# Sparse layer of a fused two-block network: inner rows and second weights as scaled 2-byte pairs, rows turned by DMA, tiles in two halves

## The reference

```
x = x + L0_xattn(layernorm(x), ctx)
xf = layernorm(x)                                   # 2048 x 512
inter = xf @ c1_w.T @ c2_w.T                        # 512 -> 16 -> 1792
idx = argmax of each block of 32 columns of inter   # 56 blocks a row
h = relu(xf . w1[idx])                              # one kept number per block
x = x + sum over the blocks of h * w2t[idx]
x = x + L1_xattn(layernorm(x), ctx)
x = x + L1_gated_ffn(layernorm(x))
```

## Time and profile before

| | |
|---|---|
| median of three runs | 1622.94 us |
| the profiled execution | 1623.3 us, of which the span from first to last instruction is 1621.5 us |
| granted TensorE clock, mean | 0.987 of full speed |
| TensorE matmul busy | 1553.2 us (96%) |
| VectorE busy | 1175.9 us (73%) |
| ScalarE busy | 812.9 us (50%) |
| GpSimd busy | 597.4 us (37%) |
| first attention (with the layer's first matmuls) | 0 to about 183 us |
| sparse layer, TensorE | about 183 to 553 us |
| second attention and gated layer | 554 to 1621.5 us |

### The profile page before, as it was taken

How to read it: one execution, slowest core, us unless ns; L and a number is a source line. 1 busy time by engine, 2 the same in 40 slices (tenths; PEclk the granted TensorE clock), 3 DMA queues, 4 the chain that set the end, 5 groups by cost and what they waited for, 6 DMA issues and landing times.

```text
span 1621.5 us, 28847 instructions
## 1 busy us (share of the span) xinstructions
PE 1553.2 (96%) x11178; PEld 970.2 (60%) x11178; DVE 1175.9 (73%) x2200; ACT 812.9 (50%) x2496; POOL 597.4 (37%) x570
## 2 busy tenths in 40 slices
PE   5999799999999878999999999999999999999998
PEld 4878566767666644555555655655555555555554
DVE  4886787878877768767667667667667667667777
ACT  5678411010011465656646656656656656656753
POOL 5668641212212133333324334334333333334343
PEclk9999899999999989999999999999999999999999
DMA  7432130000000121122121121121122122111102
GB/s 232 155 112 92 65 143 1 1 1 0 1 1 1 54 59 46 34 85 57 29 61 50 31 66 51 29 66 53 29 64 57 29 61 56 30 27 31 24 21 105
DMA packets 124073, 85.45 MB, mean 53 GB/s; under 512 B 108592, under 2 KB 108720, under 8 KB 121248
## 3 DMA queue, kind: packets, MB, share of 16 engines
q1 hardware_dynamic: 122640, 76.27, 17.4%
q10 hardware_dynamic: 1296, 7.34, 1.3%
HBM read 54.22 MB, written 4.19 MB: 36 GB/s over the span
## 4 chain that ended last, share of the span: by engine, by line
PE 44%; DVE 8%; ACT 8%; DMA 3%; POOL 2%; issue 1%; DVEq 0%
PE bank L73 13%; PE bank L75 13%; PE bank L74 13%; ACT a_prob L1632 5%; DMA a_pT_lo<-a_p_lo 3%; PE bank L2239 2%; ACT bank L1603 1%; POOL a_prob L1509 1%; DVE a_qT_lo L1836 1%; DVE a_p_lo L1889 1%; PE bank L2213 1%; DVE x_res L1832 1%; DVE a_nmx L1877 1%; DVE a_q_lo L1841 1%; PE bank L2214 1%
## 5 line engine op out<-in xcount | busy, mean ns | idle before, releaser
L1632 ACT ACTIVATE a_prob<-a_prob,a_nmx 128x64 f32<-128x64 f32 x512 | 170.2, 333 | 232.9 <-DVE a_nmx L1877 232.9
L73 PE MATMUL bank<-w,a_oT_hi 128*128 128x512 f16 x512 | 196.7, 384 | 7.0 <-DVE a_oT_lo L1895 6.9
L74 PE MATMUL bank<-w,a_oT_lo 128*128 128x512 f16 x512 | 196.5, 384 | 0.0
L75 PE MATMUL bank<-w,a_oT_hi 128*128 128x512 f16 x512 | 196.3, 383 | 0.0
L1832 DVE SCALAR_TENSOR_TENSOR x_res<-bank,a_oinv,x_res 128x512 f32<-128x512 f32 x128 | 95.7, 748 | 132.6 <-PE bank L75 132.4
L73 PE MATMUL bank<-a_big 128*128 128x512 f32 (+1 forms) x416 | 166.5, 400 | 13.2 <-DVE a_big L729 8.5
L1017 ACT CAST a_big<-bank 128x512 fp32r<-128x512 f32 x64 | 34.0, 532 | 270.3 <-PE bank L1194 270.2
L1509 POOL TENSOR_TENSOR a_prob<-a_prob,a_mask 128x512 f32<-128x512 f32 x64 | 79.9, 1271 | 240.6 <-DVE a_prob L1871 240.6
L75 PE MATMUL bank<-a_big 128*128 128x512 f32 (+1 forms) x416 | 157.3, 378 | 0.0
L975 POOL TENSOR_TENSOR a_wide<-a_wide 128x448 bf16<-128x448 bf16 x64 | 66.4, 1037 | 246.4 <-DVE a_wide L1064 246.4
L74 PE MATMUL bank<-a_big 128*128 128x512 f32 (+1 forms) x416 | 156.7, 377 | 0.0
(11 more groups left out here) (342 smaller groups left out, 4261.2 us busy)
## 6 DMA issues: line engine op xcount, KB each, us to landing
shared<-in_l_wq SPq DMA_DIRECT2D x8, 1024.0 KB, 4.9
shared<-in_l_wo SPq DMA_DIRECT2D x8, 1024.0 KB, 5.2
shared<-in_w ACTq DMA_DIRECT2D x8, 896.0 KB, 4.5
a_wide<-in_l_ctxT SPq DMA_DIRECT2D x16, 256.0 KB, 2.8
x_res<-in_x SPq DMA_DIRECT2D x16, 256.0 KB, 4.0
shared<-in_ctx SPq DMA_DIRECT2D x16, 256.0 KB, 3.7
shared<-in_l_wkv SPq DMA_DIRECT2D x8, 512.0 KB, 3.9
out_x<-x_res SPq DMA_DIRECT2D x16, 256.0 KB, 2.1
```

The costliest lines, as they stand in the source:

```text
L73: pe.matmul(out, a_hi, b_hi, start=first, stop=False)
L74: pe.matmul(out, a_lo, b_hi, start=False, stop=False)
L75: return pe.matmul(out, a_hi, b_lo, start=False, stop=last)
L1632: ins = act.activation(pt, pt, ACT.Exp, bias=nmx[:, col:col + 1], accum_out=den[:, col:col + 1])
```

## The change

1. h is no longer split after the turning but before it: ScalarE makes a 2-byte high part from h in SBUF (`hidden_hi`), GpSimd the low part (`hidden_lo`), and SP turns both with DMA transposes of 128 x 896 (`hidden_T`), two halves of a tile, so four a tile. The 14 TensorE transposes, the copy out of PSUM and VectorE's low part go.
2. w2 becomes a scaled 2-byte pair. Its largest magnitude is found during the first attention: w2 is loaded once more in 7 pieces (SP), VectorE reduces one piece in each of bodies 6 to 12, spreads and turns the maximum in bodies 12 and 13 (one TensorE transpose) and makes the scale. Each piece then gets a scaling pass on ScalarE before its split; pieces 0 and 1 are scaled and split in front of the last exponential of the first attention.
3. The next chunk's rows are normalised and cut into 2-byte pairs in SBUF (ScalarE, GpSimd) and turned by SP's DMA transposes, one tile at a time (`rows_T`, `rows_hi`, `rows_lo`). The 16 TensorE transposes a chunk and VectorE's `dve_norm` and `dve_lo` for them go. `low_rank` runs per tile of 128 columns instead of per chunk.
4. TensorE's order: a tile has two halves, two quarters of hidden, then a half of the previous product with w2, then two score matmuls (loop below). The four banks freed give hidden three banks instead of two.
5. Scales: xf in this layer is scaled by 4 and w1 to 8 instead of 1024 and 16384, so that h fits 2 bytes; the second attention keeps its own.
6. The loads of the next layer's weights are issued after tile 1's transposes, in the same SP queue.

```diff
-        w2_hi, w2_lo = l0.big[:, 0:NI * D], l0.big[:, NI * D:2 * NI * D]
+        w2_hi, w2_lo = sb("w2_hi", [P, NI * D], F16), sb("w2_lo", [P, NI * D], F16)
+        hT_hi, hT_lo = sb("hT_hi", [P, NI, P], F16), sb("hT_lo", [P, NI, P], F16)
+        h_hi, h_lo = sb("h_hi", [P, INTER], F16), sb("h_lo", [P, INTER], F16)
+        xr_hi, xr_lo = sb("xr_hi", [P, TPC, D], F16), sb("xr_lo", [P, TPC, D], F16)
-        i_banks, h_banks, hT_banks, o_banks = bank[0:2], bank[2:4], bank[4:6], bank[6:8]
+        i_banks, h_banks, o_banks = bank[0:2], bank[2:5], bank[6:8]
 # SP
+            def hidden_T(n, e):
+                if n:
+                    sp.wait_ge(s_og, 2 * (n - 1) + e + 1)
+                sp.wait_ge(s_hh, n * NQ + 2 * e + 2)
+                sp.dma_start_transpose(hT_hi[:, e * NH:(e + 1) * NH, :], h_hi[:, half_cols(e)]).then_inc(s_hT[e], 16)
+                sp.wait_ge(s_hl, n * NQ + 2 * e + 2)
+                sp.dma_start_transpose(hT_lo[:, e * NH:(e + 1) * NH, :], h_lo[:, half_cols(e)]).then_inc(s_hT[e], 16)
+            def rows_T(c, t):
+                k, rows = c * TPC + t, slice(t * P, (t + 1) * P)
+                if k:
+                    sp.wait_ge(s_xT, 32 * k)
+                sp.wait_ge(s_h, (k + 1) * NQ)
+                sp.wait_ge(s_xrh, k + 1)
+                sp.dma_start_transpose(m.xT_hi[:, :, rows], xr_hi[:, t, :]).then_inc(s_xT, 16)
+                sp.wait_ge(s_xrl, k + 1)
+                sp.dma_start_transpose(m.xT_lo[:, :, rows], xr_lo[:, t, :]).then_inc(s_xT, 16)
+            for n in range(NT):
+                c, t = n // TPC, n % TPC
+                hidden_T(n, 0)
+                if t == TPC - 2:
+                    rows_T(c, 0)
+                    rows_T(c, 1)
+                if t == TPC - 1:
+                    rows_T(c, 2)
+                hidden_T(n, 1)
+                if t == TPC - 1:
+                    rows_T(c, 3)
+                if n == 1:
...
 # GpSimd
+            def hidden_lo(n, q):
+                if n:
+                    pool.wait_ge(s_hT[q // 2], 32 * n)
+                pool.wait_ge(s_hh, n * NQ + q + 1)
+                pool.tensor_tensor(h_lo[:, quarter(q)], h[:, quarter(q)], h_hi[:, quarter(q)], ALU.subtract).then_inc(s_hl, 1)
...
 # ScalarE
+            def hidden_hi(n, q):
+                if n:
+                    act.wait_ge(s_hT[q // 2], 32 * n)
+                act.wait_ge(s_hm, n * NQ + q + 1)
+                act.copy(h_hi[:, quarter(q)], h[:, quarter(q)]).then_inc(s_hh, 1)
...
 # VectorE
+            for n in range(NT):
+                c, t = n // TPC, n % TPC
+                select(n, 0)
+                select(n, 1)
+                if TPC <= n + 1 < NT:
+                    low_lo(n + 1, bass.ts((n + 1) % TPC, P), low_bank[32:64, 0:P])
...
+                if 2 <= n < NT - 1:
+                    add_out(n - 1)
+                find_max(n, 2)
+                find_max(n, 3)
...
+                select(n, 2)
+                select(n, 3)
+                if n + 1 < NT:
+                    find_max(n + 1, 0)
+                    find_max(n + 1, 1)
 # TensorE
+            for n in range(2, NT - 1):
+                hidden(n, 0)
+                hidden(n, 1)
...
+                if n + 1 >= TPC:
+                    low_rank(n + 1)
+                out_half(n - 1, 1)
+                block_scores(n, 2)
+                block_scores(n, 3)
...
+                hidden(n, 2)
+                hidden(n, 3)
+                block_scores(n + 1, 0)
+                block_scores(n + 1, 1)
...
+                out_half(n, 0)
 # the first attention
+            if n in MAX2_AT:
+                w2_largest(MAX2_AT[n])
+            if n == 12:
+                w2_spread()
+            if n == 13:
+                w2_scales()
+            if n == NT - 1:
+                before_exps()
```

More of the change, by code:

```diff
@@ L266, in l0_attention @@
     MAX_AT = {n: n - 1 for n in range(1, 5)}
+    MAX2_AT = {n: n - 6 for n in range(6, 13)}
     SPLIT_AT = {n: n - 7 for n in range(7, 15)}
@@ L1186, in _ @@
+            ins.then_inc(m.wql_ok, 1)
+            add_out(NT - 1)
         @block.tensor
         def _(pe):
[L1188 to L1195 removed]
@@ L1197, in out_rows, with block_scores @@
-            def out_rows(n, g, odd, free=True, split=False):
-                pe.wait_ge(s_hTl, n * NQ + g + 1)
-                if split:
-                    pe.wait_ge(wl_ok, -(-TG[g].stop * D // PW))
-                if free and g == 0:
+            def block_scores(n, q):
+                if q == 0:
+                    pe.wait_ge(s_lowl, low_turn(n))
+                if n or q >= 2:
+                    pe.wait_ge(s_eq, n * NQ + q - 1)
+                pe.matmul(i_banks[q % 2][:, 0:QC], low[:, bass.ts(n % TPC, P)], c2st[:, quarter(q)], start=True,
+                          stop=True).then_inc(s_i, 1)
@@ new lines, in hidden @@
+            def hidden(n, q):
+                e, rows = n * NQ + q, bass.ts(n % TPC, P)
+                if n >= TPC and q == 0:
+                    pe.wait_ge(s_xT, 32 * (n - TPC + 1))
+                if e >= 3:
+                    pe.wait_ge(s_hm, e - 2)
+                elif e == 1:
+                    pe.wait_ge(s_lowl, 1)
+                for k in range(KD):
+                    ins = split_mm(pe, h_banks[e % 3][:, 0:QC], m.xT_hi[:, k, rows], m.xT_lo[:, k, rows],
+                                   w1_hi[:, k, quarter(q)], w1_lo[:, k, quarter(q)], k == 0, k == KD - 1)
+                ins.then_inc(s_h, 1)
@@ new lines, in low_rank, with out_half @@
+            def low_rank(n):
+                rows = bass.ts(n % TPC, P)
+                pe.wait_ge(s_xT, 32 * (n - TPC + 1))
+                if n > TPC:
+                    pe.wait_ge(s_lowl, low_turn(n) - 1)
+                for k in range(KD):
+                    ins = split_mm(pe, low_bank[0:RK3, 0:P], c1_hi[:, k, :], c1_lo[:, k, :], m.xT_hi[:, k, rows],
+                                   m.xT_lo[:, k, rows], k == 0, k == KD - 1)
+                ins.then_inc(s_low, 1)
+            def out_half(n, e):
+                pe.wait_ge(s_hT[e], 32 * (n + 1))
+                if n == 0:
+                    pe.wait_ge(wl_ok, (4, NP)[e])
+                if n >= 2 and e == 0:
@@ L1208, in out_rows @@
                                    j == 0, j == NI - 1)
                 ins.then_inc(s_og, 1)
-            def block_scores(c, t, n, q, before, first):
-                cols = slice(q * QC, (q + 1) * QC)
-                if t == 0 and q == 0:
-                    pe.wait_ge(s_lowl, c + 1)
-                if before or q >= 2:
-                    pe.wait_ge(s_eq, n * NQ + q - 1)
-                pe.matmul(i_banks[q % 2][:, 0:QC], low[:, t * P:(t + 1) * P], c2st[:, cols], start=True, stop=True).then_inc(s_i, 1)
```

519 lines of the change are left out of this document (273 added, 246 removed).

## The result

The changed kernel takes 1573.96 us (median of 4 runs, 1573.62 to 1577.21), the kernel before beside it 1622.24 (1617.17 to 1624.62): a ratio of 0.9711 with a 95% interval of 0.9684 to 0.9738. That is 48 us faster; forecast were 37 (1586, range 1572 to 1607). The result lies inside the range, 2 us above its lower end. The profiled execution took 1573.65 us, its span is 1571.9.

What follows compares the result with a forecast made beforehand. TensorE, busy 22.00 of 22 us in the sparse layer, was taken as the bound; its list of 317.2 us plus waits of 8, 2 and 3 gave -40, first attention +3, so 1586 us, range 1572 to 1607.

Steps and rivals of the forecast that it cites:

- The bound: Sparse layer's steady part: only TensorE's list counts, busy 22.00 of 22 us; a tile was to take 20.1 us.
- The list: TensorE's work in the sparse stage after the change, priced per instruction from trace rows: 317.2 us in all.
- Waits at the start: TensorE's waits in the stage: 8 us in the first two tiles, 2 at tile 2, 3 for other small ones.
- The loads ahead of tile 2: Next layer's 4.5 MB stand before tile 2's transposes in one queue; TensorE waits 0 to 5 us, taken as 2.
- The pieces of w2: Stage start: the second half of tile 0's product waits for split w2 pieces until about 211 us.
- The turned half: Each half tile: turned h lands at U + 16.1, needed at U + 20.7 (U: scores start), so 4.6 us spare.
- The other half has the same distance: Second half of each tile: its turned h was to have the same 4.6 us to spare as the first.
- VectorE's last h follows 0.6 later: Each half tile: VectorE finishes the last h 0.6 us after TensorE's two quarters of hidden are done.
- Rival A: Turned halves come slightly late; TensorE waits 0.7 us at each of 32 halves: +22, 1608 us; chance 0.13.
- The end of the stage: After the last hidden quarter, 13.6 us of product cover its turning (about 7 us) and the next layer's weights and rows.
- rival B: VectorE bounds the tile: each marks instruction stretched to 2.80 us makes 23.3 a tile; 1620 to 1630 us; chance 0.05.
- First attention: VectorE's added reductions for w2's maximum, 8.5 us plus some 2 of small ones, cost 0 to 10, taken as 3.

## Why the prediction came out right, and what of it did not

- **The bound: right.** The tile is TensorE's list. The fourteen transposes added to it came back at full price; doubled DMA transposes and doubled GpSimd work made a steady tile 0.8 us longer.
- **The list: 317.2 forecast, 311.7 with the measured prices.** Hidden and w2 were exact (143.6 and 145.2; 0.216). The score pairs took 32 x 0.42 = 13.4 for 15.4, low_rank 144 x 0.056 = 8.0 for 11.5: the lower bound of its range, in proportion to the columns, was the value. A tile was 19.7 for 20.1. Of the 41 us, 10.0 are the w2 products and 19.6 the transposes of h, each with a run behind it. The rest is estimated from rows alone: 5.6 for the transposes of rows and 64 x 0.29 - 13.4 = 5.2 for scores in pairs, 40.4 in all.
- **Waits at the start: 13 forecast, 17.2 measured** (328.9 - 311.7). The trace lists 12.6: 7.2 in the first two tiles for 8, 4.58 at tile 2 for 2, 0.85 in the last tile for 3. The other 4.6 are a remainder, and the half clock explains about 4 of it: the matmuls of 207.6 to 210.7 and of 240.1 to 244.9 us ran at the 1.2 GHz level. The forecast knew of it in the earlier trace rows and left it out of the sum. That this and the list's error cancelled is luck: the stage came out within 1.3 us of a sum with two terms wrong by 4 to 6 us each.
- **The loads ahead of tile 2: place and cause right, size not.** 2 us were taken of 0 to 5; it was 4.58 and the slow stretch. Spreading them gave 7.9 in the median and 7.2 in the stage.
- **The pieces of w2:** until about 211 forecast, 207.6 and 209.8 in the two profiles of the changed kernel.
- **The turned half: in time, for partly wrong reasons.** An issue took 1.22 to 1.30 us, not 2.08: 4 blocks take 1.20. The landing was 3.0. The cover of 4.6 held for first halves and not for second ones. In the fence, the last hidden matmul and the last h of a first half, then of the second:

```profile
369.37 0.35 PE L77 MATMUL bank<-w,xT_hi 128*128 128x448 f16 x1
369.81 0.62 DVE L1216 SCALAR_TENSOR_TENSOR h<-bank,a_wide 128x448 f32<-128x448 f32 x1 [0.44 <-PE bank L77]
...
379.55 0.35 PE L77 MATMUL bank<-w,xT_hi 128*128 128x448 f16 x1
...
382.28 0.62 DVE L1216 SCALAR_TENSOR_TENSOR h<-bank,a_wide 128x448 f32<-128x448 f32 x1
```

  The first half's low part is issued at 372.43, landed at 375.4 and used at 380.15: 4.7 us of cover, found in most first halves (2.9 to 4.3 in the others, mostly beside the turning of rows). The second's is issued at 384.90, landed at 387.9 and used at 389.90: 2.0, and 2.0 to 2.8 in most second halves (1.1 at least). "The other half has the same distance" was the faulty step, and so was "VectorE's last h follows 0.6 later" for that half. There no half product lies between the scores and hidden, so VectorE is still behind: h starts 2.73 us after the last hidden matmul in place of 0.44. In addition one pair of scores less (0.4 us) stands before its product. The doubled transposes waited at exactly these second halves. Rival A's wait at each of 32 halves did not come: behind tile 2 the trace lists one, of 0.85 us.
- **The end of the stage: nearly.** The forecast let all 13.6 us of product behind the last hidden quarter cover its turning (about 7). Only the first two of the three half products, 9 us, stand before the use of the last half. Its turning took 10.0 us (493.3 to 503.35), and TensorE waited 0.85.
- **VectorE (rival B): covered with much to spare.** The marks took 0.71 to 0.72 us in the mean of the steady part (0.644 before) and 1.61 at most; 18.5 us a tile had been allowed for, and VectorE is busy 77 of 100 us between 300 and 500, 15.2 a tile.
- **The third bank:** the text said that TensorE could run four quarters ahead with it. It can, and gains nothing.
- **First attention: +3 forecast, none measured.** Its bodies 1 to 15 take 131.84 us after and 131.76 before, from the exponentials' starts.
- **The 11 us between the forecast saving (37) and the measured one (48):** 3 are the attention, 1 to 3 the stage. The remaining 5 to 7 are not explained by a mechanism; they are within what comparisons scatter, since the second one, on another chip, gave 44.
- **The range:** the lower end, -13, was to stand for a head without waits together with cheap narrow matmuls; its own terms make 13 and 8. Of the 8 came 5.5; the waits were there in full. That the result lies just above 1572 is therefore the attention and the scatter, and not that case.

Left open: the one long run of the doubled transposes, and why the part behind the stage varies between 1064 and 1068.5 us. No run took the transposes of rows or the pairing of scores alone.

## What to carry to other kernels

Where one engine is busy all the time, price its list per instruction from rows and trust it; here two experiments (one thing made cheaper, one put back) came within 0.3 and 3 us of their terms. The rest of the time is at the ends of the stage: there the long waits (3.3 and 4.6 us) cost themselves and the half clock behind them, and moving one wait only helped when the queue of the engine behind it was moved as well. A slack has to be reckoned for each half by itself, with the engine that is last there. A large load should not stand ahead of a small urgent transfer in the same queue; spread, the same bytes left no wait in the traces.

## What the runs showed of the hardware

- A DMA transpose holds SP 1.22 to 1.30 us for seven 128 x 128 blocks and 1.20 to 1.27 for four; they land after 3.0 and 2.4 to 2.5. Two or three fly at once without slowing each other (3.0 to 3.1 at an issue distance of 1.34).
- Behind 4.5 MB of loads the issue itself stalls: 6.71 and 2.88 us on SP, landing after 10.8 and 5.6.
- float32 transposes of 128 columns take 0.109 us each in a row of fourteen, and 0.35 for four with a score behind them, 0.0875 each.
- A wait of 4.6 us left TensorE at the 1.2 GHz level for its next matmuls (0.43 instead of 0.216 from start to start, for 4.8 us); taking it away gave 7.2 us in the stage. Shorter waits went both ways: behind 2.5 us the clock of 182 to 205 us was 1.00 in the first profile of the changed kernel, behind 2.3 us it was 0.93 in the second.
